# Searched instruction orders of a two-layer conv kernel: another set of tables, 221 instead of 267 identity products

## What is computed

```python
# layer 0: window attention (8x8 windows, 4 heads), a gated 1x1, a 3x3 convolution
scores = einsum('bhnd,bhmd->bhnm', q, k) / sqrt(d) + bias
out = einsum('bhnm,bhmd->bhnd', softmax(scores), v)           # then proj, added to x
a, b = split(w1 @ x + w1_b); g = edge_pad(a * sigmoid(b))
x = x + leaky_relu(conv3x3(g, w2) + w2_b)
# layer 1: depthwise 3x3, layer norm, gated linear attention with rope, depthwise 3x3, MLP
x = x + dwconv(x, cpe1);  n = layernorm(x)
act = silu(act_proj @ n); t = silu(dwconv(in_proj @ n, dwc))
q, k = elu(qk @ t) + 1;   z = 1 / (q . mean(k) + 1e-6)
kv = rope(k)^T t / n_px;  y = rope(q) kv * z + dwconv(t, lepe)
x = x + out_proj @ (y * act);  x = x + dwconv(x, cpe2)
x = x + fc2 @ gelu(fc1 @ layernorm(x))
```

## Time and profile before

| | before |
|---|---|
| median of three launches | 854.25 us |
| profiled launch | 852.0 us, of which the program's span is 850.2 us |
| PE (TensorE) busy | 761.1 us, 90% |
| PE weight loads | 478.3 us, 56% |
| DVE (VectorE) busy | 547.1 us, 64% |
| ACT (ScalarE) busy | 496.7 us, 58% |
| POOL (GpSimd) busy | 299.2 us, 35% |
| granted TensorE clock, mean | 0.943 of full |

### The profile page before, as it was taken

How to read it: one execution, slowest core, us unless ns; L and a number is a source line. 1 busy time by engine, 2 the same in 40 slices (tenths; PEclk the granted TensorE clock), 3 DMA queues, 4 the chain that set the end, 5 groups by cost and what they waited for, 6 DMA issues and landing times. The chain is left out here.

```text
span 850.2 us, 19878 instructions
## 1 busy us (share of the span) xinstructions
PE 761.1 (90%) x8514; PEld 478.3 (56%) x8514; DVE 547.1 (64%) x698; ACT 496.7 (58%) x675; POOL 299.2 (35%) x215
## 2 busy tenths in 40 slices
PE   4799998799889998899899998799799988888997
PEld 3688455586635555576454444486454434775644
DVE  3878125999875125989994136999974018895702
ACT  3475258767252668878553588966442588333146
POOL 2232031274940220246950220498510200785200
PEclk9899999999989996989899999999789998896999
DMA  2200120000002100000011110100001101000101
GB/s 60 46 3 1 30 58 1 2 2 15 2 2 43 55 17 1 16 15 16 1 26 33 43 29 1 30 15 3 15 15 29 30 1 29 15 1 1 30 15 43
DMA packets 34345, 16.77 MB, mean 20 GB/s; under 512 B 27120, under 2 KB 34160, under 8 KB 34258
## 3 DMA queue, kind: packets, MB, share of 16 engines
q1 hardware_dynamic: 32450, 15.28, 7.3%
q10 hardware_dynamic: 1808, 0.22, 0.2%
HBM read 4.87 MB, written 3.54 MB: 10 GB/s over the span
## 5 line engine op out<-in xcount | busy, mean ns | idle before, releaser
L1288 POOL TENSOR_TENSOR SC<-SC,mx 128x768 f32<-128x768 f32 x48 | 77.8, 1621 | 229.4 <-DVE mx L1096 229.3
L568 PE MATMUL ps<-ZP,wdw 48*64 48x384 f32 x1728 | 143.8, 483 | 1.2 <-ACT QH L990 0.8
L1163 DVE SCALAR_TENSOR_TENSOR CT<-TP,vec_sb,CT 112x768 f32<-112x768 f32 x96 | 130.2, 1368 | 1.3
L1149 DVE SCALAR_TENSOR_TENSOR QS<-ZP,vec_sb,QS 112x768 f32<-112x768 f32 x96 | 109.3, 1163 | 0.6
L568 PEld LDWEIGHTS ps<-ZP,wdw 48*64 48x64 f32 x1728 | 66.2, 133 | 72.2 <-issue 65.0
L1135 DVE TENSOR_TENSOR LV<-LV,XB 112x768 f32<-112x768 f32 x24 | 24.7, 1030 | 98.5 <-ACT LV L942 98.5
L659 PEld LDWEIGHTS ps<-vx,PT 128*128 128x128 f32 x576 | 71.6, 204 | 13.3 <-issue 5.9
L659 PE MATMUL ps<-vx,PT 128*128 128x52 f32 x576 | 74.2, 288 | 3.1 <-DVE KX L1170 1.2
L568 PE MATMUL ps<-G,w_sb 48*64 48x384 f32 x864 | 74.2, 494 | 1.9 <-ACT G L907 0.9
L815 PEld LDWEIGHTS ps<-ident_sb 128*128 128x128 f32 x534 | 64.7, 197 | 19.2 <-issue 12.2
L815 PE MATMUL ps<-ident_sb 128*128 128x128 f32 x534 | 71.2, 287 | 2.7 <-DVE XB L1221 1.4
(11 more groups left out here) (173 smaller groups left out, 1383.4 us busy)
## 6 DMA issues: line engine op xcount, KB each, us to landing
XR<-in_x_dram SPq DMA_DIRECT2D x48, 72.0 KB, 2.0
YB<-YF SPq DMA_DIRECT2D x48, 72.0 KB, 2.2
ZP<-XB SPq DMA_DIRECT2D x48, 72.0 KB, 2.3
out_dram<-XB SPq DMA_DIRECT2D x24, 144.0 KB, 2.2
rope_th_sb<-in_rope_th_dram SPq DMA_DIRECT2D x1, 441.0 KB
w_sb<-in_w_dram SPq DMA_DIRECT2D x2, 81.0 KB
wfc_sb<-in_wfc_dram SPq DMA_DIRECT2D x4, 36.0 KB
wln_sb<-in_const_dram SPq DMA_DIRECT2D x6, 9.0 KB
```

The source lines that it names most:

```text
L568: mm = pe.matmul(slot(job)[half(c, HALF), r * BANK:r * BANK + SPX], w[half(r), tap * HALF:(tap + 1) * HALF], shifted(t, d * CROWS + c * WI ...
L1149: dve.scalar_tensor_tensor(out=rows16(T0[n]), in0=win, scalar=wt, in1=rows16(T0[n]), op0=ALU.mult, op1=ALU.add).then_inc(dwc_step, 1)
L1163: dve.scalar_tensor_tensor(out=ct, in0=win, scalar=wt, in1=ct, op0=ALU.mult, op1=ALU.add).then_inc(lepe_step, 1)
L1288: pool.tensor_tensor(sc, sc, bc_last(mx[:, (u % NSC) * 12:(u % NSC) * 12 + 12], TOK), ALU.subtract).then_inc(sub_ready, 1)
```

## The change

Only the five tables differ. The same jobs stand in them, 491 on PE, 444 on ACT, 481 on DVE, 108 on POOL and 54 on SP, in other orders and with other slots. The sum of the +m goes from 267 at 37 places to 221 at 29 places (so the tables say, the 322 of the change's short title is not the count of this kernel before). The number of activation table loads stays at 91. All functions are word for word the same, one line up, since PE_ORDER has a line less. The first line of PE_ORDER, and the line that holds the last rows of POOL's rope for pair 2:

```diff
-    v.0.0@0 v.0.1@1 s1.0.0@2+8 qk.0.0@3 sc0.0.0@0+11 sc1.0.0@1 qk.0.1@2 sc0.0.1@3+12 tr0.0.0@0+4 sc1.0.1@1
+    v.0.0@0 v.0.1@1 s1.0.0@2+9 qk.0.0@3 sc0.0.0@0+8 sc1.0.0@1 qk.0.1@2 sc0.0.1@3+14 tr0.0.0@0+1 sc1.0.1@1
...
-    qs.2.1 su1.3.4 qs.2.2 su0.3.5 su1.3.5 ym.2.0 ym.2.1 ym.2.2 x2.3.0 x2.3.1 x2.3.2 kr.3.0 qc.3.0 qs.3.0 kr.3.1
...
+    qs.2.0 su1.3.5 qc.2.1 qc.2.2 qs.2.1 ym.2.0 qs.2.2 ym.2.1 ym.2.2 x2.3.0 x2.3.1 x2.3.2 kr.3.0 qc.3.0 kr.3.1
```

More of the change, by code:

```diff
@@ L67 @@
[L67 to L71, removed]
@@ L77 @@
[L77 to L81, removed]
@@ new lines @@
+    v.2.1@3 sc0.2.0@1 va2.0.1@2 d0.1.0@0 tr0.2.0@3 sc1.2.0@1 xc.1.0@2 qk.2.1@0 d0.1.1@3 va.1.0@2 tr1.2.0@1
+    sc0.2.1@0 xc.1.1@3 d0.1.2@2 va.1.1@1 av.2.0@3 tr0.2.1@0 xc.1.2@2 ip.1.0@1 ip.1.1@0 va.1.2@3 ot.2.0@2
+    sc1.2.1@1 qk.2.2@0 f12.0.0@3 pj.2.0@2 v.2.2@1 ip.1.2@2 f11.0.0@3 ac.1.0@1 xc2.0.2@2 sc0.2.2@0 va2.0.2@2
+    f2.0.0@3 f10.0.1@1 f12.0.1@0 sc1.2.2@3 qk.2.3@2 f11.0.1@3 ac.1.1@0 ac.1.2@1 f2.0.1@3 f10.0.2@2 f12.0.2@3
+    f11.0.2@0 w1.2.0@2 f2.0.2@3 vt.1.0@0 kt.1.0@1 tr1.2.1@2 sc0.2.3@3 q.1.0@0 av.2.1@2 tr0.2.2@1 vt.1.1@0
@@ L107 @@
+    q.3.2@0 kv.3.2@2+33 kp.3.0@3+8 kk.3.0@1+2 dn.3.0@0 dn.3.1@2 at.3.0@3 at.3.1@1 dn.3.2@0 at.3.2@3+4 op.3.0@2
+    op.3.1@1+3 d3.3.0@0+25 op.3.2@3 xc2.3.0@2 va2.3.0@1+1 f10.3.0@0+8 f11.3.0@3 d3.3.1@2 d3.3.2@1 xc2.3.1@0
+    f12.3.0@3 xc2.3.2@2 va2.3.1@1 f2.3.0@0 va2.3.2@3 f10.3.1@2+3 f12.3.1@0 f11.3.1@1 f2.3.1@3+6 f10.3.2@2
+    f12.3.2@0 f11.3.2@1 f2.3.2@3
 """
 ACT_ORDER = """
[L110 to L111 removed]
@@ new lines @@
+    yn2.0.1 sb1.2.0 qb.2.1 sb0.2.1 yn.1.0 yn.1.1 ob.2.0 c10.1.0 sb1.2.1 yn.1.2 x1.2.0 qb.2.2 c11.1.0 c12.1.0
+    c13.1.0 c10.1.1 c14.1.0 c11.1.1 c15.1.0 sb0.2.2 o.0.0 c16.1.0 sb1.2.2 c17.1.0 qb.2.3 c18.1.0 yn2.0.2 c12.1.1
+    o.0.1 c13.1.1 c10.1.2 c14.1.1 c11.1.2 c15.1.1 c12.1.2 c16.1.1 c13.1.2 g.2.0 c17.1.1 o.0.2 c18.1.1 c14.1.2
+    c15.1.2 ko.1.0 c16.1.2 qo.1.0 c17.1.2 ob.2.1 c18.1.2 sb0.2.3 c20.1.0 c20.1.1 c21.1.0 x1.2.1 ks.1.0 c22.1.0
+    c21.1.1 c23.1.0 ko.1.1 ob.2.2 ko.1.2 sb1.2.3 qb.2.4 x1.2.2 c24.1.0 c22.1.1 ks.1.1 sb0.2.4 qb.2.5 sb1.2.4
@@ new lines @@
+    ks.1.2 c23.1.1 kp.1.0 sb0.2.5 qo.1.1 ob.2.3 c24.1.1 kk.1.0 c25.1.0 c25.1.1 ob.2.4 x1.2.3 sb1.2.5 c26.1.0
+    c26.1.1 az.1.0 x1.2.4 c27.1.0 c27.1.1 c28.1.0 c28.1.1 g.2.1 am.1.0 ob.2.5 g.2.2 az.1.1 qo.1.2 x1.2.5 am.1.1
+    g.2.3 oz.1.0 c20.1.2 g.2.4 c21.1.2 c22.1.2 c23.1.2 c24.1.2 oz.1.1 c25.1.2 c26.1.2 c27.1.2 c28.1.2 az.1.2
+    am.1.2 g.2.5 oz.1.2 yn2.1.0 qb.3.0 yn2.1.1 yn2.1.2 sb0.3.0 sb1.3.0 yn.2.0 qb.3.1 yn.2.1 sb0.3.1 c10.2.0
+    c11.2.0 yn.2.2 ob.3.0 c12.2.0 c13.2.0 c14.2.0 c10.2.1 c15.2.0 sb1.3.1 x1.3.0 c16.2.0 qb.3.2 c17.2.0 c11.2.1
```

206 lines of the change are left out of this document (98 added, 108 removed).

## The result

The changed kernel is slower. Four launches took 867.14 to 879.42 us, median 873.21, against 854.84 for the kernel before: a ratio of 1.0226, 95% interval 1.014 to 1.0312. The forecast was 851.6 us and no change, in a range of 842.5 to 863.0. (Medians and ratios leave out launches more than 1.5% above the fastest of their kernel, which here are two of e5's four and two of e11's ten.)

What follows compares the result with a forecast made beforehand. PE and DVE were taken to bound the kernel in alternating stretches. Terms 3.1 + 0.2 - 5.4 - 0.5 = -2.6 us gave 849.4 against the profiled 852.0; with the median 2.25 higher, 851.6 us, range 842.5 to 863.

Steps and rivals of the forecast that it cites:

- A: Pair 0's start: moved jobs delay ip.0.1 by 12.1 us, DVE is relieved of 8.9; az.0.0 +3.1 us.
- The count: Whole kernel: 46 fewer identity products, 12.3 us of PE's busy time, nearly all where PE waits anyhow.
- B: Pair 1: taps begin earlier, DVE gets more work, PE waits anew at kv.1.0; +0.2 us in sum.
- C: Pair 2: PE's wait at kk.2.0 goes, az.2.0 and then oz.2.2 come earlier; -5.4 us.
- D: Last pair: POOL's hole before kr.3.1 closes, kr.3.2 waits about 1.6 us; -0.5 us in sum.
- The clock rival: Fewer products let more stretches fall to 1.2 GHz; three more make +10 us, 859 to 862; chance 0.10.
- The lock rival: Pair 0's taps: DVE and POOL exclude each other, the stretch shrinks 3 us, not 8.9; total 857.7; chance 0.14.
- The rope rival: Pair 2: az.2.0 stays at 620.0, POOL's ropes end late, +5.9 us for -5.4; total 863; chance 0.12.

Runs made afterwards that it cites:

- e5: The change with set-up jobs s2.0.0 and s3.0.0 moved back to a late place on PE and DVE: 872.34 us, ratio 1.0196.
- e11: The kernel before with z0.0.0 first on DVE and, in pair 2, x1.3.3 and kk.2.0 early: 852.06 us, ratio 0.9945.
- e14: The change's lists up to 58 us, then the order of the kernel before for the jobs left: 868.07 us, ratio 1.0175.
- e3: The change with the identity products of the kernel before at six start places, 43 for 32: 875.48 us, ratio 1.0238.
- e17: Lists of the kernel before up to 62 us, then e5's order for the jobs left: 870.28 us, ratio 1.0174.
- e4: The kernel before with the change's identity products at six start places, 32 for 43: 858.96 us, ratio 1.0051.
- e15: The kernel before without the 42 identity products from cv.0.1 to cv.3.1: 861.60 us, ratio 1.0083.
- e8: The kernel before without the 182 identity products of the last pair, from ip.3.1 on: 858.26 us, ratio 1.0038.
- e1: The change's lists up to op.0.0, then those of the kernel before: 876.82 us, ratio 1.0250.
- e7: The kernel before with x1.3.3 and kk.2.0 moved up on DVE in pair 2: 851.68 us, ratio 0.9956.
- e9: The change with the zeroing job z0.0.0 moved to the front of DVE's list: 870.36 us, ratio 1.0173.
- e10: The kernel before with the zeroing job z0.0.0 moved to the front of DVE's list: 853.53 us, ratio 0.9975.

## Why the prediction was wrong, point by point

**A, mis-sized by 13.0.** The step that failed is that the first 60 us were costed at nothing, and that jobs put into a full PE stretch were thought to bring their own time and no more. The moved jobs themselves measured 15.2 us (forecast 14.2), and the relief of DVE 8.1 (forecast 8.9): that arithmetic held. What lacked is 6.6 us of low clock by `ip.0.1` (1.7 more behind it are in the 8.1) and 5.5 us of waits, 1.8 of them in the first 62 us and 3.7 in the stretch that the prediction held to be full. e14 shows that the start alone, its order with its eleven products fewer, makes the low clock; by e3 the old products don't take it away in that order. But the start is not all of it: e17, with the old start, has `az.0.0` 17 us late and not 3, so the moved jobs cost far more than their own time too, in waits (5.9 us, 2.3 of them at its joint) and low clock (3.7). The forecast read the order of `cv.0.0` and what stands behind it, and not the first three strips, where `s2.0.0`, `ot`, `pj` and `tr` had changed places too. 

**The count.** "Nearly all stand where PE waits anyhow" was true and the conclusion false. A product in a wait costs nothing and buys clock: e4, e15 and e8 price them at 0.34, 0.16 and 0.02 us each. The change took 11 from the start, 4 from the middle and 31 from the last pair. By e4 the eleven are worth up to 3.7 us, and e3 says that in the new order they would not have bought it.

**B, right within 3.** The new wait at `kv.1.0` came, 1.39 us (forecast 2.3), released by POOL's rope as said. Timeline of PE:

```profile
383.68 1.57 PE L742 MATMUL ps<-KX,VT 98*64 98x144 f32 x22 [1.39 <-POOL KX L1261]
```

**C, right up to `az.2.0`, wrong behind it.** PE has no wait of note at `kk.2.0`, and `az.2.0` starts 7.8 us behind the end of `kp.2.0` (forecast 9.3, before 23.3). Then it fails, in DVE's, POOL's, PE's and ACT's timelines of the change:

```profile
617.86 0.95 DVE L1206 TENSOR_TENSOR QH<-ps,QH 112x768 f32<-112x768 f32 x1
...
621.93 8.71 DVE L1162 SCALAR_TENSOR_TENSOR CT<-TP,vec_sb,CT 112x768 f32<-112x768 f32 x4
630.56 2.22 DVE L1210 TENSOR_TENSOR CT<-CT,QH 112x768 f32<-112x768 f32 x1
632.71 2.55 DVE L1162 SCALAR_TENSOR_TENSOR CT<-TP,vec_sb,CT 112x768 f32<-112x768 f32 x1
635.19 0.63 DVE L1107 RECIPROCAL rs<-ps 64x24 f32<-64x24 f32 x2
...
621.23 1.48 POOL L1272 TENSOR_TENSOR LV<-QH,rope_y_sb 112x768 f32<-112x768 f32 x1 [9.77 <-DVE QH L1175]
...
636.92 0.86 PE L666 MATMUL ps<-ident_sb,OB 128*112 128x128 f32 x3 [4.86 <-DVE OB L1112]
...
643.20 1.62 PE L685 MATMUL ps<-XR,wsq_sb 113*112 113x384 f32 x2
...
646.18 1.28 ACT L901 ACT_TABLE_LOAD   x1 [4.61 <-PE ps L686]
...
649.28 0.90 ACT L981 ACTIVATE QH<-ps,masks_sb 112x768 f32<-112x768 f32 x1
...
651.15 0.96 DVE L1206 TENSOR_TENSOR QH<-ps,QH 112x768 f32<-112x768 f32 x1
...
663.86 1.02 DVE L1214 SCALAR_TENSOR_TENSOR XB<-ps,vec_sb,XB 112x768 f32<-112x768 f32 x1 [4.15 <-PE ps L557]
```

DVE reaches `ob.3.5` at 635.2 behind taps that take 2.2 to 2.6 us beside the ropes. PE waits 4.86 us for it at `ot.3.5`, at the low clock from 633.7 to 647.4. `w1.3.4` ends at 646.1, `sg.3.4` needs it, and `z.2.2` stands behind `sg.3.4`. The ropes were done at 641.0, where the prediction had looked for the limit and priced it right within 1.2 us (19.8 us for 18.6). I had followed the chain that was named for `az.2.2` and not the attention's chain beside it. The wait of 5.32 us before went to another place at nearly its size, and the low clock with it. The VectorE and GpSimd rule of the Trainium skill ("SBUF — State Buffer", section "Who interferes with whom") names this cost; the trace agrees: the tap at 632.71 took 2.55 us beside a rope, and six took 6.28 with POOL idle in the kernel before.

**D, the mechanism right.** The hole before `kr.3.1` closed and `kr.3.2` waits 1.76 us (forecast 1.6). The tail came out 1.1 us longer and not 0.5 shorter, within its bounds.

```profile
753.94 1.01 POOL L1254 TENSOR_TENSOR KX<-KX,rope_th_sb 98x384 f32<-98x384 f32 x1
...
771.98 1.73 POOL L1254 TENSOR_TENSOR KX<-KX,rope_th_sb 98x384 f32<-98x384 f32 x1 [1.76 <-DVE KX L1169]
```

**The rivals.** The clock rival, at 0.10 and at 859 to 862, named the clock rightly, but looked for it behind new waits in the middle and gave the fewer products as its reason, which by e3 are not what keeps it low in the new order. Between the profile and the median lie another 6 us: the four launches went with a mean clock of 0.933, 0.925, 0.926 and 0.916 at 867.1, 870.6, 875.8 and 879.4 us. The lock rival did not come: by it the stretch behind `ip.0.1` would have shrunk by 3 us, and it shrank by 8.1 (8.8 between e14 and e1). The lower bound of A's range was read off DVE, its upper (12.1) off work alone; neither could hold 16.1. The rope rival's own steps (643.4, 8 and 3.5 us) give 654.9 and not 655.8, which changes nothing.

## What stays open

Why the clock rises at 43 to 47 us and stays, in the order of before, and comes late or falls again in the order of the change, is not settled. The seven profiles with the changed start had 20 to 48 us at the low clock ahead of 90 us (without e5's slowest launch 20 to 31), those with the old one 7 to 14. Nor was it tried whether e7 gains more with `sb1.3.5` moved up as well. Products, set-up jobs and zeroing are excluded as the sole cause. Which of the swapped jobs it is was not tried one by one, and why the two halves don't add was not taken apart either. Each kernel has one profile, while the launches of the change differ by 12 us, so a difference of a few us between two profiles is not shown by them alone.

## What to carry to other kernels

Read the first microseconds of a reordered program as closely as the places where engines are full: lists that only swap small jobs there and drop eleven fillers cost 11 us. Value a filler by the clock of what stands behind its wait, and test it by taking it out in groups. A wait removed at one job is worth its time only if every chain that ends at the same place (here the ropes, `ob` to `z`, and the clock) is followed to its end.

## What the runs showed of the hardware

TensorE can be busy, as the profile counts it, at 1.2 GHz without the clock rising: 13.60 us of 13.60 in e14, 13.70 of 13.70 in e9. It also fell at 36.5 us in e10 and at 36.3 in e9, where PE had stood 1.16 and 0.35 us in the seven us ahead. The Trainium skill ("TensorE: Matmul & The Clock Gate", section "HAM oscillation — how this bites in real kernels") ties the low clock to gaps in which PE waits. The waits of 4.86 us in the change and of 2.91 and 2.36 in e15 agree; the start does not, since a busy PE stayed low there.
